# Attention kernel with one in-order DMA queue: three kinds of transfers moved or reordered between SyncE and ScalarE

## The chip, the core and the metric

The kernel runs on one core of one Trainium2 chip. The metric is the device time of one execution in microseconds (us). A measurement of this kernel can tell about 0.5% from no change.

## What is computed

A transformer block on 2 sequences of 1024 rows of width 512, fp32, cut here to its skeleton:

```python
mod = silu(c) @ wmod                      # shift, scale, gate of both halves
h = layernorm(x) * (1 + ca) + sa
q, k, v = h @ Wq, h @ Wk, h @ Wv          # 32 query heads, 8 key/value heads, head size 64
q, k = rope(q), rope(k)
attn = softmax(causal(q @ k.T / 8)) @ v
x = x + ga * (attn @ Wo)
h = layernorm(x) * (1 + cb) + sb
gu = h @ ternary(w_gate_up).T             # ternary weights: per group of 64, sign times scale
x = x + gb * (rms_norm(silu(gate) * up) @ ternary(w_proj).T)
```

## The kernel before

The program has four stages, one after the other, each with its own instruction streams for the five engines: a prologue (layer norm, modulation), `attention`, the output projection and the feed-forward part. The change lies in `attention` (line 343 and following).

`attention` computes one group of 4 query heads and one key/value head at a time, 8 groups (g = 0 to 7). A group has 72 steps (T), and in each step TensorE (PE) does one tile of 128 keys by 4 heads of 128 queries: it turns (transposes) the exponentials (line 698, four of 128 columns), and multiplies, two steps later (`LAG = 2`), the high and low halves with the values (lines 710, 711). In the same steps it projects the next queries, keys and values (lines 656 to 658) and computes scores (lines 688 to 690). The engines are kept in step only by semaphores; each engine's stream is written out by a `step` function, in which every kind of work has a fixed delay in steps behind the event that it belongs to. An engine works strictly through its own stream, so a wait on a semaphore holds back all that stands behind it on that engine.

**Query pieces.** A group needs eight pieces of rotated queries (`X_USES`, kinds `qx` and `qy`). A piece that starts at step s is projected in steps s to s+3; VectorE (DVE) multiplies by cosine and sine at s+4 (lines 835, 836); SyncE (SP) swaps the halves by four transfers at s+5 (`swap`, line 572); GpSimd (POOL) adds at s+6 (line 898); ScalarE (ACT) rounds at s+8 (line 792), POOL takes the rest at s+8 (line 909); SP places the result in `q_hl` by four transfers at s+10 (`place`, line 582). The pieces that the first scores of the next group need start at steps 46 and 51 (here called piece 9 and piece 10, their numbers in `X_USES`), so piece 10 is placed at step 61, and the scores at step 63 wait for it. Piece 11 starts at 56 and is swapped at step 61 too, ahead of the place of piece 10.

**Output blocks.** Each pair of steps' rows gives a large and a small block of outputs, 16 blocks of 4 heads by 128 queries in a group. A block whose last tile is at step e is copied by ACT at e+2 (`copy_out`, line 748), its upper half is shifted to the lower partitions by SP at e+3 (`shift`, line 558), added by POOL at e+5 (line 889), multiplied by the reciprocal denominators by POOL at e+6 (line 894), and stored by SP at e+7 (`store`, line 566). Blocks 10 and 11 end at steps 51 and 53.

**Reciprocals.** For a pair n of blocks, DVE makes the reciprocals at step 9n and turns them at 9n+1; SP saves them to memory at 9n+2 (`save_den`, line 589, four transfers) and loads them spread over 64 partitions into `rd_all` (`spread_den`, line 595) once per block. `rd_all` holds one block. So the load of a block can only start when the block before has been multiplied; the order of SP's stream ensures that, since the load stands right behind the store of the block before, and that store waits for the multiplication.

**Ternary weights.** 6 units in a group: loaded by ACT's queue (line 800), worked on by ACT, DVE and POOL, and stored by SP at 12 steps behind the unit's start (`store_unit`, line 600), after POOL's last operation on it (line 924) at 11.

SP's stream in a step (lines 602 to 622) has the order shift, swap, place, store, save, spread of the large block, spread of the small block behind a store, ternary store, and the weights of the next group once.

Of the kernel before, what the change touches and what calls it, by code (L numbers as in the profile page):

```python
# [20 lines left out]
ALU = mybir.AluOpType  # L21
ACT = mybir.ActivationFunctionType
AX = mybir.AxisListType
F32 = mybir.dt.float32
# [3 lines left out]
P = 128  # L28
B, S, E = 2, 1024, 512
T = B * S  # L30
H, KVH, D = 32, 8, 64
GQ = H // KVH
# [262 lines left out]
LAG = 2  # L295
# [47 lines left out]
def attention(nc, wq, wk, wv, w_gu, w_p, consts_in, w_in, w_raw, cos, sin, mask, ident, hT_hi, hT_lo, ot_dram, rden_dram,  # L343
              tern_gu, tern_p):
    with ExitStack() as ctx:
        sb = lambda n, s, d: ctx.enter_context(nc.sbuf_tensor(n, s, d))
# [15 lines left out]
        p_lo = sb("p_lo", [P, P_RING, 512], F32R)  # L362
        o_sb = sb("o_sb", [P, 2, 512], F32)
        o_low = sb("o_low", [D, 2, 512], F32)
        rd_all = sb("rd_all", [D, 512], F32)
        negm = sb("negm", [P, len(ROWS)], F32)
        den = sb("den", [P, 2, len(ROWS)], F32)
        rd = sb("rd_b", [P, 2, DEN_COLS], F32)
# [163 lines left out]
        def unit_of(g, u, gu, down):  # L532

            if u < 4:
                return gu[bass.ds(g, 1), u].rearrange("g p d -> (g p) d")
            return down[bass.ds(g, 1), u - 4].rearrange("g p r h -> (g p) r h")

        def unit_tile(u, tile):

            return tile[:] if u < 4 else tile[:].rearrange("p (r h) -> p r h", r=2)  # L540
# [9 lines left out]
        @block.sync  # L550
        def _(sp):
            ot_g = ot_dram.rearrange("(g h d) t -> g d h t", g=KVH, h=GQ)
            tern_gu_g = tern_gu.rearrange("(g u p) d -> g u p d", g=KVH, p=P)
            tern_p_g = tern_p.rearrange("(u r p) (g h) -> g u p r h", u=2, p=P, g=KVH)

            def shift(g, n):
                blocks_o.await_(sp, g, n)
                sp.dma_start(o_low[:, n % 2, :], o_sb[D:P, n % 2, :]).then_inc(o_shifted[n % 2], 16)

            def store(g, n):  # L560
                pair, small = divmod(n, 2)
# [29 lines left out]
            def spread_den(g, n):  # L591
                if n % 2 == 0:
                    pairs_out.await_(sp, g, n // 2)
                row = rden_dram[n // 2 % 2, GQ * (n % 2):GQ * (n % 2) + GQ, :].rearrange("(o h) q -> o (h q)", o=1)
                sp.dma_start(rd_all[:], row.broadcast_to([D, GQ * P])).then_inc(rd_in[n % 2], 16)

            def store_unit(g, u):
                to = unit_of(g, u, tern_gu_g, tern_p_g)
                units_tern.await_(sp, g, u)
                sp.dma_start(to, unit_tile(u, w_hat)).then_inc(tern_out, 16)  # L600

            def step(body, T):
                for g, n in body.blocks(T, LAG + 1):
                    shift(g, n)
                for g, n, _ in body.uses(T, 5, kinds=("kv", "qx", "qy")):
                    swap(g, n)
                for g, n, _ in body.uses(T, 10, kinds=("qx", "qy")):
                    place(g, n)
                for g, n in body.blocks(T, LAG + 5):
                    store(g, n)  # L610
                for g, n in body.pairs(T, 2):
                    save_den(g, n)
                for g, n in body.pairs(T, 6):
                    spread_den(g, 2 * n)
                for g, n in body.blocks(T, LAG + 5):
                    if n % 2 == 0:
                        spread_den(g, n + 1)
                for g, u in body.units(T, 12):
                    store_unit(g, u)
                if T == W_LOAD and body.holds(0, 0, KVH - 2):  # L620
                    sp.wait_ge(w_ready, body.g + 1)
                    load_weights(sp, wq, wk, wv, w_raw, w_in, body.g + 1)
# [109 lines left out]
        def _(act):  # L732
# [3 lines left out]
            act.copy(ident_r[:], ident[:]).then_inc(consts_ready, 1)  # L736
            act.copy(mask_r[:], mask[:]).then_inc(consts_ready, 1)

            def high(g, T):
                tiles_t.await_(act, g, T)  # L740
                tiles_pv.await_(act, g, T - P_RING)
                act.copy(p_hi[:, T % P_RING, :], ps[:, T_BANK + T % 2, :]).then_inc(phi_ready, 1)  # L742
# [15 lines left out]
            def step(body, T):  # L758
# [8 lines left out]
                    high(g, t)  # L767
                for g, n in body.blocks(T, LAG):
                    copy_out(g, n)
                for g, r in body.rows(T, 1):  # L770
                    exponentials(g, r)
                for g, n, _ in body.uses(T, 4, kinds=("kv",)):
# [20 lines left out]
                for g, u in body.units(T, 3):  # L793
                    units_in.await_(act, g, u)
                    units_tern.await_(act, g, u - 1)
                    act.activation(w_abs[:], wf[:], ACT.Abs).then_inc(abs_ready, 1)
                    act.activation(w_sign[:], wf[:], ACT.Sign).then_inc(sign_ready, 1)
                for g, u in body.units(T, 0):
                    units_sign.await_(act, g, u - 1)
                    act.dma_start(unit_tile(u, wf), unit_of(g, u, gu_g, wp_g)).then_inc(wf_in, 16)  # L800

            bodies(act, step)

# [76 lines left out]
        def _(pool):  # L881
# [4 lines left out]
            def step(body, T):  # L886
# [4 lines left out]
                for g, n in body.blocks(T, LAG + 4):  # L891
                    blocks_a.await_(pool, g, n)
                    blocks_rd[n % 2].await_(pool, g, n // 2)
                    pool.tensor_tensor(o_sb[0:D, n % 2, :], o_sb[0:D, n % 2, :], rd_all[:], ALU.mult).then_inc(o_scaled, 1)  # L894
                for g, n, _ in body.uses(T, 6, kinds=("kv", "qx", "qy")):
                    rows, buf = D if X_USES[n][0] == "kv" else P, buf_of(n)
                    buf_swap[buf].await_(pool, g, BUF[buf].index(n))
# [662 lines left out]
```

## Time and profile before

| | us |
|---|---|
| median of 3 runs | 2027.5 |
| lowest and highest | 2020.21, 2028.98 |
| the profiled execution | 2022.91 |
| its span, first to last instruction | 2021.1 |
| PE busy | 1783.6 |
| DVE busy | 1277.2 |
| ACT busy | 1148.7 |
| POOL busy | 952.4 |

The mean granted TensorE clock of the profiled execution is 0.961 of full speed (2.4 GHz). The attention stage's matmuls run from about 68 us to 1388 us of the span. "Idle before" in a row is the time in which the engine had nothing to do ahead of the instruction, and the name behind the arrow is what released it. A line's number is that of the kernel before. In rows, SPq and ACTq are the queues of SP and ACT on which transfers are issued; an issue also shows the time its engine's sequencer takes for it.

### The profile page before, as it was taken

The page shows a single profiled execution, that of the slowest core. Times are in us where ns is not written, and L with a number is a line of the kernel's source. Part 1 is how long each engine was busy: PE and PEld are TensorE (multiplying, and loading weights), DVE is VectorE, ACT ScalarE, POOL GpSimd, SP SyncE. Part 2 cuts the span into 40 slices and gives each one's busy share as a digit, 9 for nine tenths or more (in the row PEclk, how much of TensorE's full clock was granted, in tenths as well). Part 3 has the DMA queues.
Part 4 walks back from the last instruction along what each step waited for, and adds up shares of the span by engine and source line. Part 5 has one row for each costly group of instructions (what it writes and reads, how often), then busy time and mean ns, then how long its engine had stood idle before and what let it go on. Part 6 is the DMA issues. An engine that isn't in the chain of part 4 may idle for free. (4 is left out here: it accounts for less than half of the span.)

```text
span 2021.1 us, 28183 instructions
## 1 busy us (share of the span) xinstructions
PE 1783.6 (88%) x9585; PEld 1482.5 (73%) x9585; DVE 1277.2 (63%) x2079; ACT 1148.7 (57%) x2307; POOL 952.4 (47%) x773
## 2 busy tenths in 40 slices
PE   7489989989889989998998998984999789999997
PEld 6267867878778778777877877873788667777776
DVE  6368768768768767776876876884333255454443
ACT  4257767767767767776776776784322244323221
POOL 0235656566556656655665656654000024444443
PEclk9799999999989989999998999997999989999999
DMA  6134344244334434433434334333655300101000
GB/s 247 27 84 111 86 116 105 80 115 112 82 97 111 104 89 105 123 81 103 117 83 118 101 81 117 96 95 118 225 178 190 116 22 1 48 0 48 1 26 22
DMA packets 174921, 190.96 MB, mean 94 GB/s; under 512 B 31408, under 2 KB 117688, under 8 KB 174784
## 3 DMA queue, kind: packets, MB, share of 16 engines
q1 hardware_dynamic: 156992, 164.07, 29.0%
q10 hardware_dynamic: 17792, 25.17, 4.2%
q8 instruction: 73, 1.20, 0.3%
q14 instruction: 64, 0.52, 0.1%
HBM read 86.12 MB, written 31.74 MB: 58 GB/s over the span
## 5 line engine op out<-in xcount | busy, mean ns | idle before, releaser
L812 DVE TENSOR_TENSOR p_lo<-ps_b,p_hi 128x512 fp32r<-128x512 f32 x576 | 395.0, 687 | 181.0 <-ACT p_hi L742 177.0
L742 ACT CAST p_hi<-ps_b 128x512 fp32r<-128x512 f32 x576 | 338.0, 589 | 218.1 <-PE ps_b L698 213.9
L755 ACT ACTIVATE p<-ps_b,negm 128x640 f32<-128x640 f32 (+7 forms) x512 | 382.6, 751 | 127.1 <-DVE negm L820 123.2
L820 DVE TENSOR_REDUCE negm<-ps_b 128x1 f32<-128x640 f32 (+7 forms) x512 | 377.4, 747 | 113.4 <-PE ps_b L690 111.0
L698 PE MATMUL ps_b<-ident,p 128*128 128x128 f32 x2304 | 356.5, 278 | 9.6 <-DVE p_lo L812 3.8
L688 PE MATMUL ps_b<-k_hh,q_hl 128*128 128x512 f32 (+3 forms) x768 | 271.7, 354 | 81.6 <-DMA q_hl<-rot_x 53.0
L710 PE MATMUL ps_b<-p_hi,v_hl 128*128 128x512 f32 x576 | 278.1, 483 | 11.7 <-ACT o_sb L748 11.2
L698 PEld LDWEIGHTS ps_b<-ident,p 128*128 128x128 f32 x2304 | 253.8, 142 | 40.2 <-issue 11.5
L689 PE MATMUL ps_b<-k_l,q_hl 128*128 128x512 f32 (+3 forms) x768 | 260.7, 352 | 0.0
L894 POOL TENSOR_TENSOR o_sb<-o_sb,rd_all 64x512 f32<-64x512 f32 x128 | 163.7, 1279 | 166.9 <-DMA rd_all<-reciprocals 164.9
L688 PEld LDWEIGHTS ps_b<-k_hh,q_hl 128*128 128x128 f32 x768 | 147.9, 193 | 126.5 <-issue 56.2
L711 PE MATMUL ps_b<-p_lo,v_hl 128*128 128x512 f32 x576 | 229.2, 398 | 0.0
L1294 PE MATMUL ps_d<-h_hi,gu 128*128 128x512 f32 x512 | 201.4, 393 | 8.1 <-ACT xn_d L1313 4.6
L1295 PE MATMUL ps_d<-h_lo,gu 128*128 128x512 f32 x512 | 200.0, 391 | 0.0
L656 PE MATMUL ps_b<-hT_hi,w_hi 128*128 128x512 f32 x384 | 159.2, 414 | 45.9 <-DVE v_hl L847 16.3
L898 POOL TENSOR_TENSOR rot_c<-rot_c,rot_x 128x512 f32<-128x512 f32 (+1 forms) x96 | 122.9, 1280 | 151.9 <-DMA rot_x<-rot_s 151.8
L889 POOL TENSOR_TENSOR o_sb<-o_sb,o_low 64x512 f32<-64x512 f32 x128 | 164.2, 1287 | 40.4 <-DMA o_low<-o_sb 40.2
L689 PEld LDWEIGHTS ps_b<-k_l,q_hl 128*128 128x128 f32 x768 | 148.2, 193 | 29.5
L1380 POOL TENSOR_TENSOR sq<-a 128x512 f32<-128x512 f32 x60 | 71.2, 1186 | 179.1 <-DVE a L1462 178.7
L657 PE MATMUL ps_b<-hT_hi,w_lo 128*128 128x512 f32 x384 | 155.5, 405 | 0.0
L658 PE MATMUL ps_b<-hT_lo,w_hi 128*128 128x512 f32 x384 | 153.8, 401 | 0.0
L1462 DVE TENSOR_TENSOR a<-ps_d,sg 128x512 f32<-128x512 f32 x64 | 44.2, 691 | 159.4 <-PE ps_d L1295 140.9
(139 smaller groups left out, 3344.3 us busy)
## 6 DMA issues: line engine op xcount, KB each, us to landing
rot_x<-rot_s SPq DMA_DIRECT2D x320, 64.0 KB, 2.0
q_hl<-rot_s SPq DMA_DIRECT2D x128, 128.0 KB, 2.4
q_hl<-rot_x SPq DMA_DIRECT2D x128, 128.0 KB, 2.4
rd_all<-reciprocals SPq DMA_DIRECT2D x128, 128.0 KB, 3.0
o_low<-o_sb SPq DMA_DIRECT2D x128, 128.0 KB, 2.3
attention_out<-o_sb SPq DMA_DIRECT2D x128, 128.0 KB, 2.4
o_raw<-attention_out SPq DMA_DIRECT2D x32, 512.0 KB, 4.7
wf<-in_L_ffn_w_gate_up ACTq DMA_DIRECT2D x32, 256.0 KB, 3.3
```

The costliest lines, as they stand in the source:

```text
L688: pe.matmul(ps[:, bank, 0:n], q, k_hh[:, unit, k0:k0 + n], start=True, stop=False)
L689: ins = pe.matmul(ps[:, bank, 0:n], q, k_l0[:, unit, k0:k0 + n], start=False, stop=(k0 + n < nk))
L698: ins = pe.transpose(ps[:, T_BANK + T % 2, h * P:(h + 1) * P], p_32[:, parity, h, column * P:(column + 1) * P], ident[:])
L710: pe.matmul(ps[:, O_BANK, :], v_hl[:, unit, j, :], p_hi[:, T % P_RING, :], start=(j == 0), stop=False)
L711: pe.matmul(ps[:, O_BANK, :], v_hl[:, unit, j, :], p_lo[:, T % P_RING, :], start=False, stop=(j == i)).then_inc(pv_done, 1)
L742: act.copy(p_hi[:, T % P_RING, :], ps[:, T_BANK + T % 2, :]).then_inc(phi_ready, 1)
L755: act.activation(p_32[:, parity, h, column * P:column * P + nk], s, ACT.Exp, bias=negm[:, k:k + 1], scale=1.0, accum_out=den[:, parity, k: ...
L812: dve.tensor_tensor(p_lo[:, T % P_RING, :], ps[:, T_BANK + T % 2, :], p_hi[:, T % P_RING, :].bitcast(F32), ALU.subtract).then_inc(plo_read ...
L820: dve.tensor_reduce(negm[:, k:k + 1], s, AX.X, ALU.max, negate=True).then_inc(max_ready, 1)
L889: pool.tensor_tensor(o_sb[0:D, n % 2, :], o_sb[0:D, n % 2, :], o_low[:, n % 2, :], ALU.add).then_inc(o_added, 1)
L1294: pe.matmul(ps[:, bank + half, :], gu[:, m, half, k, :], h_hi[:, parity, k, :], start=(k == 0), stop=False)
L1295: i = pe.matmul(ps[:, bank + half, :], gu[:, m, half, k, :], h_lo[:, parity, k, :], start=False, stop=(k == CT - 1))
```

## The change

`shift` and `store_unit` are moved from SP to ACT: ACT's step issues the shift at the same step (e+3) as before, right behind its `high` and `copy_out`, and the ternary store three steps later (15 instead of 12 behind the unit's start), right behind the two activations that wait for the same unit.
```diff
-        rd_all = sb("rd_all", [D, 512], F32)
+        rd_all = sb("rd_all", [D, 2, 512], F32)
...
         @block.sync
-            def shift(g, n):
-                blocks_o.await_(sp, g, n)
-                sp.dma_start(o_low[:, n % 2, :], o_sb[D:P, n % 2, :]).then_inc(o_shifted[n % 2], 16)
...
                 if n % 2 == 0:
                     pairs_out.await_(sp, g, n // 2)
...
-                sp.dma_start(rd_all[:], row.broadcast_to([D, GQ * P])).then_inc(rd_in[n % 2], 16)
-
-            def store_unit(g, u):
-                to = unit_of(g, u, tern_gu_g, tern_p_g)
-                units_tern.await_(sp, g, u)
-                sp.dma_start(to, unit_tile(u, w_hat)).then_inc(tern_out, 16)
+                blocks_s.await_(sp, g, n - 2)
+                sp.dma_start(rd_all[:, n % 2, :], row.broadcast_to([D, GQ * P])).then_inc(rd_in[n % 2], 16)
 
             def step(body, T):
-                for g, n in body.blocks(T, LAG + 1):
-                    shift(g, n)
                 for g, n, _ in body.uses(T, 5, kinds=("kv", "qx", "qy")):
                     swap(g, n)
                 for g, n, _ in body.uses(T, 10, kinds=("qx", "qy")):
                     place(g, n)
+                for g, n in body.pairs(T, 2):
+                    save_den(g, n)
+                for k in range(2):
+                    for g, n in body.pairs(T, 5 + 2 * k):
+                        spread_den(g, 2 * n + k)
                 for g, n in body.blocks(T, LAG + 5):
                     store(g, n)
-                for g, n in body.pairs(T, 2):
-                    save_den(g, n)
-                for g, n in body.pairs(T, 6):
-                    spread_den(g, 2 * n)
-                for g, n in body.blocks(T, LAG + 5):
-                    if n % 2 == 0:
-                        spread_den(g, n + 1)
-                for g, u in body.units(T, 12):
-                    store_unit(g, u)
...
         @block.scalar
+            def shift(g, n):
+                blocks_o.await_(act, g, n)
+                act.dma_start(o_low[:, n % 2, :], o_sb[D:P, n % 2, :]).then_inc(o_shifted[n % 2], 16)
+
+            def store_unit(g, u):
+                to = unit_of(g, u, tern_gu_g, tern_p_g)
+                units_tern.await_(act, g, u)
+                act.dma_start(to, unit_tile(u, w_hat)).then_inc(tern_out, 16)
...
                 for g, n in body.blocks(T, LAG):
                     copy_out(g, n)
+                for g, n in body.blocks(T, LAG + 1):
+                    shift(g, n)
                 for g, r in body.rows(T, 1):
                     exponentials(g, r)
...
                     act.activation(w_sign[:], wf[:], ACT.Sign).then_inc(sign_ready, 1)
+                for g, u in body.units(T, 15):
+                    store_unit(g, u)
...
         @block.gpsimd
-                    pool.tensor_tensor(o_sb[0:D, n % 2, :], o_sb[0:D, n % 2, :], rd_all[:], ALU.mult).then_inc(o_scaled, 1)
+                    pool.tensor_tensor(o_sb[0:D, n % 2, :], o_sb[0:D, n % 2, :], rd_all[:, n % 2, :], ALU.mult).then_inc(o_scaled, 1)
...
-    nc = bacc.Bacc("TRN2", target_bir_lowering=False, num_devices=1)
+    nc = bacc.Bacc("TRN2", target_bir_lowering=False, num_devices=1, dynamic_dma_scratch_size=4096)
```

The first place is SP's stream from step 58 to step 61 of a group, ahead of the scores at step 63. Before, it reads (L566 block stores, L595 reciprocals, L600 ternary store, L572 swap of piece 11, L582 place of piece 10; in brackets the semaphore that it waits for, `b_o_scaled` being POOL's multiplication):

```order
L566 DMA attention_out<-o_sb 64x4x128 [waits b_o_scaled]
L595 DMA rd_all<-reciprocals 64x512
L566 DMA attention_out<-o_sb 64x4x128 [waits b_o_scaled]
L595 DMA rd_all<-reciprocals 64x512 [waits b_rd_out]
L600 DMA ternary_down<-w_hat 128x2x256 [waits b_t_tern]
L572 DMA rot_x<-rot_s 32x512 [waits b_x_used]
L572 DMA rot_x<-rot_s 32x512 x3
L582 DMA q_hl<-rot_s 64x2x256 [waits b_qlo_ready1]
L582 DMA q_hl<-rot_x 64x2x256
```

Now the same steps read (new line numbers: L560 stores, L590 reciprocals, L566 swap, L576 place):

```order
L560 DMA attention_out<-o_sb 64x4x128 [waits b_o_scaled]
L590 DMA rd_all<-reciprocals 64x512 [waits b_o_scaled,b_rd_out]
L560 DMA attention_out<-o_sb 64x4x128 [waits b_o_scaled]
L566 DMA rot_x<-rot_s 32x512 [waits b_x_used]
L566 DMA rot_x<-rot_s 32x512 x3
L576 DMA q_hl<-rot_s 64x2x256 [waits b_qlo_ready1]
L576 DMA q_hl<-rot_x 64x2x256
```

The load of block 11's reciprocals has gone to step 52, and the ternary store has left the queue; the two block stores still stand ahead of swap and place.

The second place is ACT's stream around a block's copy (here the end of the first pairs of group 0). Before (L742 `high`, L748 `copy_out`, L755 exponentials, L792 rounding):

```order
L792 CAST rot_s<-rot_c 128x512 [waits b_rotated0]
L742 CAST p_hi<-ps_b 128x512 [waits b_pv_done,b_t_ready] x2
L748 COPY o_sb<-ps_b 128x512 [waits b_o_out1,b_pv_done]
L755 ACTIVATE p,den<-ps_b,negm 128x640 [waits b_max_ready]
L742 CAST p_hi<-ps_b 128x512 [waits b_pv_done,b_t_ready]
```

Now (L738, L744, L751, L790 are the same four, L728 is the shift):

```order
L790 CAST rot_s<-rot_c 128x512 [waits b_rotated0]
L738 CAST p_hi<-ps_b 128x512 [waits b_pv_done,b_t_ready]
L728 DMA o_low<-o_sb 64x512 [waits b_o_copied]
L738 CAST p_hi<-ps_b 128x512 [waits b_pv_done,b_t_ready]
L744 COPY o_sb<-ps_b 128x512 [waits b_o_out1,b_pv_done]
L751 ACTIVATE p,den<-ps_b,negm 128x640 [waits b_max_ready]
L738 CAST p_hi<-ps_b 128x512 [waits b_pv_done,b_t_ready]
L728 DMA o_low<-o_sb 64x512 [waits b_o_copied]
```

A shift now stands directly behind a `high` of the step after its block's copy, and waits for ACT's own copy. PE's, DVE's and POOL's streams keep their order.

## Rows read from the trace of the kernel before

**Rows 1.** the page, part 1: busy us, share of the span, instructions

```profile
PE 1783.6 (88%) x9585; PEld 1482.5 (73%) x9585; DVE 1277.2 (63%) x2079; ACT 1148.7 (57%) x2307; POOL 952.4 (47%) x773
```

**Rows 2.** waits of PE: us in total, times, longest us

```profile
PE ps_b L688 <- DMA q_hl<-rot_x: 53.0, 8, 7.9
PE ps_b L688 <- ACT p L755: 28.6, 30, 2.1
```

**Rows 3.** timeline of PE at one stall: start us, us, operation, [idle before]

```profile
256.83 0.40 PE L656 MATMUL ps_b<-hT_hi,w_hi 128*128 128x512 f32 x1
...
264.89 0.77 PE L688 MATMUL ps_b<-k_hh,q_hl 128*128 128x512 f32 x1 [7.21 <-DMA q_hl<-rot_x]
```

**Rows 4.** timeline of PE, the first stall and one behind ACT

```profile
109.65 0.76 PE L688 MATMUL ps_b<-k_hh,q_hl 128*128 128x512 f32 x1 [3.25 <-DMA q_hl<-rot_x]
...
191.94 0.33 PE L688 MATMUL ps_b<-k_hh,q_hl 128*128 128x128 f32 x1 [1.98 <-ACT p L755]
```

**Rows 5.** windows: stretch, us, busy PE, PEld, DVE, ACT, POOL, PEclk, DMA

```profile
265.00:270.00 5.00, 5.00 (x16) 4.16 (x17) 2.62 (x5) 1.80 (x3) 1.26 (x1) 0.54 0.02 3
192.00:196.00 4.00, 3.53 (x23) 3.06 (x24) 2.53 (x5) 3.35 (x9) 0.01 (x1) 1.00 0.28 70
```

**Rows 6.** waits of SP's queue and of POOL

```profile
SPq L566 <- POOL o_sb L894: 214.9, 74, 5.1
...
SPq L600 <- POOL w_hat L924: 61.6, 38, 3.9
...
POOL o_sb L894 <- DMA rd_all<-reciprocals: 164.9, 49, 6.0
```

**Rows 7.** timeline of SP's DMA issues ahead of that stall

```profile
254.90 0.62 SPq L566 DMA_DIRECT2D attention_out<-o_sb  x1
...
257.27 0.41 SPq L600 DMA_DIRECT2D ternary_down<-w_hat  x1
257.73 2.47 SPq L572 DMA_DIRECT2D rot_x<-rot_s  x4
260.24 0.66 SPq L582 DMA_DIRECT2D q_hl<-rot_s  x1
...
262.28 0.61 SPq L582 DMA_DIRECT2D q_hl<-rot_x  x1
```

**Rows 8.** timeline of POOL over the same steps

```profile
253.59 1.28 POOL L894 TENSOR_TENSOR o_sb<-o_sb,rd_all 64x512 f32<-64x512 f32 x1 [2.29 <-DMA rd_all<-reciprocals]
254.84 1.29 POOL L909 TENSOR_TENSOR rot_x<-rot_c,rot_s 128x512 fp32r<-128x512 f32 x1
```

**Rows 9.** timeline of DVE, same steps

```profile
250.56 0.68 DVE L836 TENSOR_TENSOR rot_s<-ps_b,sin 128x512 f32<-128x512 f32 x1
```

**Rows 10.** DMA issues: count, KB each, median us to landing

```profile
rd_all<-reciprocals SPq DMA_DIRECT2D x128, 128.0 KB, 3.0
```

**Rows 11.** lines 558 and 800: count, ns min/median/max

```profile
L558 SPq DMA_DIRECT2D o_low<-o_sb x128: 461/503/1736, 142.6 to 1392.2; - x128
...
L800 ACTq DMA_DIRECT2D wf<-in_L_ffn_w_gate_up x32: 334/347/399, 123.5 to 1331.1; - x32
```

**Rows 12.** timeline of ACT around one issue of its queue

```profile
148.51 0.59 ACT L742 CAST p_hi<-ps_b 128x512 fp32r<-128x512 f32 x1
148.52 0.34 ACTq L800 DMA_DIRECT2D wf<-in_L_ffn_w_gate_up  x1
```

**Rows 13.** timeline of all engines, end of the attention stage

```profile
1385.71 1.28 POOL L894 TENSOR_TENSOR o_sb<-o_sb,rd_all 64x512 f32<-64x512 f32 x1 [3.46 <-DMA rd_all<-reciprocals]
...
1389.53 0.59 ACT L748 COPY o_sb<-ps_b 128x512 f32<-128x512 f32 x1 [2.99 <-DMA attention_out<-o_sb]
...
1397.94 1.25 POOL L894 TENSOR_TENSOR o_sb<-o_sb,rd_all 64x512 f32<-64x512 f32 x1 [2.29 <-DMA rd_all<-reciprocals]
1399.22 0.64 SPq L566 DMA_DIRECT2D attention_out<-o_sb  x1
...
1412.53 0.77 PE L1030 MATMUL ps_c<-wo_hi,o_hi 128*128 128x512 f32 x1 [24.48 <-DVE o_lo L1143]
```

More of the change, by code:

```diff
@@ L552, in _ @@
             ot_g = ot_dram.rearrange("(g h d) t -> g d h t", g=KVH, h=GQ)
-            tern_gu_g = tern_gu.rearrange("(g u p) d -> g u p d", g=KVH, p=P)
-            tern_p_g = tern_p.rearrange("(u r p) (g h) -> g u p r h", u=2, p=P, g=KVH)
-            def shift(g, n):
-                blocks_o.await_(sp, g, n)
-                sp.dma_start(o_low[:, n % 2, :], o_sb[D:P, n % 2, :]).then_inc(o_shifted[n % 2], 16)
             def store(g, n):
@@ L737, in _ @@
             act.copy(mask_r[:], mask[:]).then_inc(consts_ready, 1)
+            tern_gu_g = tern_gu.rearrange("(g u p) d -> g u p d", g=KVH, p=P)
+            tern_p_g = tern_p.rearrange("(u r p) (g h) -> g u p r h", u=2, p=P, g=KVH)
+            def shift(g, n):
[5 more added lines that the diff above has]
+                act.dma_start(to, unit_tile(u, w_hat)).then_inc(tern_out, 16)
             def high(g, T):
```

## The prediction

> **What bounds the kernel now.** I read the page first: PE is busy 1783.6 of 2021.1 us, 88% of the span, and every other engine at most 63% [rows 1]. So only what stops PE counts, or slows it. Next the waits of PE: in the attention stage the largest is the first score matmul of a group waiting for the placed queries, 53.0 us in 8 stalls; behind it comes the wait for exponentials, 28.6 us in 30 stalls of at most 2.1 [rows 2]. Then PE's timeline at one of the eight: PE issues its last three projection matmuls from 256.83 (one every 0.23 us) and then stands 7.21 us until 264.89 [rows 3]. The first of the eight, before any block exists, is 3.25 us [rows 4]; the other seven average (53.0 - 3.25) / 7 = 7.1. The windows show a second price: in the 5 us behind such a stall the granted clock is 0.54 with PE busy all the time, while behind a stall of 1.98 us [rows 4] it is 1.00 [rows 5]. 5 x (1 - 0.54) = 2.3 us of work are lost there.
>
> Why the queries are late is in SP's queue, read backwards from the stall [rows 7]. The last of four place transfers is issued at 262.28 and PE starts 2.61 later. The four are issued from 260.24, behind the four of a swap from 257.73. From the start of the swap to PE's start it is always 2.51 + 2.04 + 2.61 = 7.16 us. The swap's data were there at 250.56 + 0.68 = 251.24 [rows 9], so SP was 6.5 us late. It stood behind a block store until 254.90 and behind a ternary store until 257.27. The block store waited for POOL's multiplication, which began at 253.59 after 2.29 us without work, waiting for the reciprocals [rows 8]; and these could be asked for only once the single buffer was free. Over the span SP waits 214.9 us for that multiplication and 61.6 for the ternary units, and POOL waits 164.9 us for reciprocals [rows 6], whose transfer takes 3.0 [rows 10].
>
> **The change, part by part.**
>
> *Reciprocals early, two buffers.* 128 loads stay 128. Block 11's now starts at step 52 instead of 58, so the multiplication at step 59 finds it. It starts at 253.59 - 2.29 = 251.30 and ends at 252.58 instead of 254.87. Nothing else on POOL changes; the remainder of piece 10 (line 909) ends at about 253.8, before the place needs it. The load's new wait, for the block two before, lies in SP's queue too: the multiplication that it wants is one to five steps older, so I cost it at nothing; what covers it is POOL's slack, and if POOL is late, swap and place are late by the same.
>
> *Ternary store off SP.* It was issued at 257.27, 1.1 us after the store from 254.90 and the load behind it (0.62 us each to issue) were through [rows 7]. On ACT it stands three steps later, right behind an activation that waits for the same unit, so it adds no wait there.
>
> *New start of the swap.* The block store (0.65 us to issue) now follows the multiplication: 252.58 + 0.65 = 253.2. Then PE starts at 253.2 + 7.16 = 260.4. Without the stall PE would start at 264.89 - 7.21 = 257.7. That leaves 2.7 us. Bounded from below by the data alone, 251.24 + 7.16 = 258.4, it leaves 0.7. POOL also waited for reciprocals in the steps before, so the multiplication should come a little sooner than 251.30; I take 2.0. From above, the stall could stay 7.2 if SP still comes late by another wait.
>
> *Sum at the stalls.* 7 x (7.1 - 2.0) = 36 us. A stall of 2.0 is like the one of 1.98 behind which the clock was full [rows 5], so 7 x 2.3 = 16 us of slow clock go too. The first stall of 3.25 has no block or ternary store ahead of it in SP's queue and stays.
>
> *The end of the stage.* The last multiplication but two waited 3.46 us for its reciprocals; the last copy of a block waited 2.99 us for the store behind it; and the last multiplication waited 2.29, before the last store at 1399.22 [rows 13]. The output projection cannot start earlier, its first matmul has 24.48 us of idle ahead. 2.99 + 2.29 = 5 us go; the bounds are 2.3 and 8.
>
> *Shifts and stores on ACT.* 128 shifts at 0.50 us (the median on SP) and 48 ternary stores at 0.41 [rows 7, 11] are 64 + 20 = 84 us of ACT's sequencer, 10 us in a group of some 162. The nearest rows are ACT's own issues of weight loads: 0.35 us [rows 11], issued 0.01 us after a `high` of 0.59 us has started [rows 12], so the issue is over before the engine is. A shift stands in the same place, behind a `high`, and 0.50 is still below 0.59; its semaphore, ACT's own copy of the step before, is long there. I take 3 us for all 176. The bounds are 0 and 84.
>
> *What comes late next.* With the long stall gone, ACT and DVE lose the pause in which they catch up, just where the widest rows (1024 columns) begin. The waits for exponentials are 28.6 / 8 = 3.6 us a group; I let them grow by 1 us a group, 7 us in all. The bounds are 0 and 3.6 x 7 = 25.
>
> The sum is 36 + 16 + 5 - 3 - 7 = 47 us. Against the profiled execution, 2022.9, that is 1976. The median of the three runs, 2027.5, lies 4.6 above that execution, within the spread shown; I put the median after at 1978, a little above the sum.
>
> **A rule that speaks against it.** Of the waits of SP's queue the rows say that 276 us hung on POOL [rows 6] and only parts of a microsecond on each issue. The Trainium skill ("DMA: Bandwidth & Descriptors", section "Issuing engines are not separate DMA queues") says that transfers issued from several engines run on the same 16 DMA engines and that spreading them saves only the sequencer's time to issue. By the rule alone this change would be worth next to nothing; I forecast more because what leaves the queue here is mostly waiting, which the rule does not speak of.
>
> **The rivals.**
>
> A. *Only issue time is saved.* SP stays late by waiting, since the two block stores and a load with a wait still stand ahead of the swap, and only two issues leave steps 58 to 61: at 0.41 and 0.62 us [rows 7] 1.0 us a group, 7 us in all. For it speaks the order of the stream; against it that the multiplication was idle for reciprocals 2.29 us in just this place. It gives 2016, no change that can be told. The rule above would have this outcome. Chance 0.09.
>
> B. *The stall shrinks by half and the clock still falls.* POOL works nearly without a pause in these steps, and a late `save_den` holds the load of step 59 and with it the store. A stall of about 4.5 gives 7 x 2.6 = 18 us, the clock nothing (behind the first stall of 3.25 I cannot exclude it), the end 5 us, ACT -3: 2003. Chance 0.15.
>
> C. *ACT's queue becomes the bound, slower.* If the issue is not hidden, each shift delays the exponentials behind it and the next `high`, and PE waits for both. The price is up to 84 us against the 54 that the rest gives before ACT and the catching up; it decides from 54 / 176 = 0.31 us exposed at each issue. Fully exposed: 2022.9 - 54 + 84 = 2053. For it speaks that PE already waits for exponentials 30 times; against it the hidden issues [rows 12]. Chance 0.08, half exposed (2011) belongs to A or B.
>
> **How the numbers follow.** The forecast has 0.68. About 0.5% (10 us) is what can be told from no change. Forecast and B are faster, 0.83; A and what C leaves in the middle are the same, 0.10; C is slower, 0.07. The range from 1957 (stall 0.7 us, no growth of other waits: 7 x 1.3 + 7 + 3 = 19 us below the sum) to 2008 takes in B and half of the bound on ACT, and leaves out A and C.
>
> **What would show it.** In the profile after: seven waits for the placed queries of 1 to 3 us each, their total with the first 15 to 25 us instead of 53.0; the windows behind them at clock 1.00; POOL's wait for reciprocals near 0; no SP wait for the ternary unit; ACT's waits by PE for exponentials 28 to 45 us; the gap before the output projection 19 instead of 24.5. I am wrong if the waits for queries stay above 35 us, or if PE's waits on ACT grow by more than they fall.

## The result and the profile after

| | before | after |
|---|---|---|
| median, us | 2026.62 | 1993.07 |
| lowest and highest, us | 2020.21, 2028.98 | 1990.73, 1994.04 |
| span of the profiled execution, us | 2021.1 | 1992.2 |

The ratio is 0.9836, 95% interval 0.9824 to 0.9848: 33.6 us faster by the medians, 28.9 by the two spans. The forecast was 1978 with a range of 1957 to 2008. The direction and the place are right, the size was forecast too large.

The page of the kernel after, part 1, against [rows 1]: every engine runs as many instructions as before, and PE's share of the span has risen from 88% to 90%. PE's busy time for the same 9585 matmuls is 4.2 us longer (1783.6 before), which bears on the clock, below.

```profile
PE 1787.8 (90%) x9585; PEld 1487.4 (75%) x9585; DVE 1277.6 (64%) x2079; ACT 1147.7 (58%) x2307; POOL 964.6 (48%) x773
```

The waits of PE over the whole span (us in total, times, longest), against [rows 2]:

```profile
PE ps_b L672 <- ACT p L751: 31.2, 34, 2.2
PE ps_b L672 <- DMA q_hl<-rot_x: 25.5, 8, 4.0
PE ps_c L1030 <- DVE o_lo L1143: 21.7, 2, 19.0
...
PE ps_b L694 <- ACT o_sb L744: 10.1, 20, 1.1
...
PE ps_b L682 <- DVE p_lo L812: 7.5, 12, 1.4
```

The wait for placed queries has halved, 53.0 to 25.5; the wait for exponentials has grown from 28.6 to 31.2, and the gap ahead of the output projection's first matmul is 19.03 instead of 24.48 [rows 13].

The same stall as in [rows 3, 7, 8], one group after the first. First SP's issues (start us, duration, line; new lines: L560 block store, L566 swap, L576 place):

```profile
252.49 0.62 SPq L560 DMA_DIRECT2D attention_out<-o_sb  x1
253.16 2.51 SPq L566 DMA_DIRECT2D rot_x<-rot_s  x4
255.71 0.77 SPq L576 DMA_DIRECT2D q_hl<-rot_s  x1
...
257.86 0.61 SPq L576 DMA_DIRECT2D q_hl<-rot_x  x1
```

POOL in the same steps (L894 multiplication of block 11, L909 remainder of piece 10), which now has no idle ahead of either:

```profile
251.16 1.31 POOL L894 TENSOR_TENSOR o_sb<-o_sb,rd_all 64x512 f32<-64x512 f32 x1
252.42 1.29 POOL L909 TENSOR_TENSOR rot_x<-rot_c,rot_s 128x512 fp32r<-128x512 f32 x1
```

And PE, with the last projection matmul and the first score:

```profile
257.40 0.39 PE L642 MATMUL ps_b<-hT_lo,w_hi 128*128 128x512 f32 x1
261.03 0.77 PE L672 MATMUL ps_b<-k_hh,q_hl 128*128 128x512 f32 x1 [3.23 <-DMA q_hl<-rot_x]
```

The multiplication runs at 251.16 instead of 253.59, the block store goes at 252.49 instead of 254.90, and no ternary store follows. The swap starts at 253.16 instead of 257.73. The stall is 3.23 us instead of 7.21. But the last place is issued at 257.86 and PE starts 3.17 us later, not 2.61 as before.

The windows behind the stalls (stretch, us, busy us of PE, PEld, DVE, ACT, POOL, granted clock, DMA, GB/s), of the kernel after:

```profile
261.00:266.00 5.00, 4.97 (x18) 4.28 (x19) 2.54 (x5) 1.93 (x3) 0.00 (x0) 0.69 0.01 3
...
736.00:741.00 5.00, 4.83 (x14) 4.09 (x15) 2.39 (x4) 1.52 (x3) 0.00 (x0) 0.50 0.00 0
```

The clock is 0.50 to 0.71 in 5 us from the start of the first score in all seven groups; before it was 0.50 to 0.71 too, with 0.50 or 0.51 in five of seven, now in two. So the slow stretch stayed although the stall halved.

The clock also falls at a second place, once in most groups: behind PE's longest wait for exponentials. Here it is in the kernel before and in the kernel after (PE's matmul behind the wait, and the 5 us from its start):

```profile
354.48 0.33 PE L688 MATMUL ps_b<-k_hh,q_hl 128*128 128x128 f32 x1 [1.97 <-ACT p L755]
354.48:359.48 5.00, 5.00 (x24) 4.47 (x25) 3.11 (x6) 3.59 (x9) 2.33 (x2) 0.66 0.20 56
```

```profile
190.97 0.33 PE L672 MATMUL ps_b<-k_hh,q_hl 128*128 128x128 f32 x1 [1.73 <-ACT p L751]
190.97:195.97 5.00, 5.00 (x24) 4.58 (x25) 2.92 (x6) 3.69 (x9) 2.14 (x2) 0.66 0.12 30
```

Before there are seven such waits of 1.96 to 2.10 us, and the clock behind them is 1.00 four times and 0.66 three times. After there are eight of 1.72 to 2.24 us, with 1.00 twice and 0.66 to 0.69 six times.

Over the span, SP's block stores wait 81.8 us for POOL's multiplication instead of 214.9 [rows 6]; the loads' new wait for an older multiplication (recorded at the helper's line, L331) adds 55.7:

```profile
SPq L560 <- POOL o_sb L894: 81.8, 53, 6.7
...
SPq L331 <- POOL o_sb L894: 55.7, 8, 7.5
```

and POOL's group of multiplications has 3.4 us of idle ahead of it, where it waited 164.9 us for reciprocals:

```profile
L894 POOL TENSOR_TENSOR o_sb<-o_sb,rd_all 64x512 f32<-64x512 f32 x128 | 163.9, 1285 | 3.4
```

ScalarE's timeline around two of the issues that it took over (ACTq is the issue, on the same time axis as the operations):

```profile
242.05 0.81 ACT L751 ACTIVATE p<-ps_b,negm 128x640 f32<-128x640 f32 x1
242.19 0.47 ACTq L728 DMA_DIRECT2D o_low<-o_sb  x1
...
256.67 0.59 ACT L738 CAST p_hi<-ps_b 128x512 fp32r<-128x512 f32 x1
256.79 0.44 ACTq L733 DMA_DIRECT2D ternary_down<-w_hat  x1
257.15 0.63 ACT L794 ACTIVATE w_abs<-wf 128x512 bf16<-128x512 f32 x1
```

The shift is issued at 242.19 for 0.47 us, while an exponential of 0.81 runs from 242.05. The ternary store is issued at 256.79 for 0.44 while a copy of 0.59 runs, and the next operation begins 0.48 after that copy began, as it would without. In these rows both are hidden, like the weight loads in [rows 12].

### The profile page after: what moved, and what is told of

Read it like the earlier page. It is cut to its first block and busy times, and to the rows that moved or that the text cites. A ratio compares the mean times of both kernels' runs of the same rounds, so it can differ in the third digit from the quotient of the medians.

```text
span 1992.2 us, 28246 instructions
## 1 busy us (share of the span) xinstructions
PE 1787.8 (90%) x9585; PEld 1487.4 (75%) x9585; DVE 1277.6 (64%) x2079; ACT 1147.7 (58%) x2307; POOL 964.6 (48%) x773
## 5 line engine op out<-in xcount | busy, mean ns | idle before, releaser
L751 ACT ACTIVATE p<-ps_b,negm 128x640 f32<-128x640 f32 (+7 forms) x512 | 381.8, 749 | 135.1 <-DVE negm L820 131.7
L738 ACT CAST p_hi<-ps_b 128x512 fp32r<-128x512 f32 x576 | 337.4, 588 | 190.5 <-PE ps_b L682 186.1
L672 PE MATMUL ps_b<-k_hh,q_hl 128*128 128x512 f32 (+3 forms) x768 | 271.0, 353 | 56.7 <-ACT p L751 31.2
L694 PE MATMUL ps_b<-p_hi,v_hl 128*128 128x512 f32 x576 | 278.5, 484 | 10.4 <-ACT o_sb L744 10.1
L898 POOL TENSOR_TENSOR rot_c<-rot_c,rot_x 128x512 f32<-128x512 f32 (+1 forms) x96 | 124.6, 1298 | 154.5 <-DMA rot_x<-rot_s 148.7
L889 POOL TENSOR_TENSOR o_sb<-o_sb,o_low 64x512 f32<-64x512 f32 x128 | 174.1, 1364 | 25.2 <-DMA o_low<-o_sb 25.0
L894 POOL TENSOR_TENSOR o_sb<-o_sb,rd_all 64x512 f32<-64x512 f32 x128 | 163.9, 1285 | 3.4
L909 POOL TENSOR_TENSOR rot_x<-rot_c,rot_s 128x512 fp32r<-128x512 f32 x64 | 82.2, 1284 | 167.7 <-ACT rot_s L790 167.7
```

The source lines that it names most:

```text
L672: pe.matmul(ps[:, bank, 0:n], q, k_hh[:, unit, k0:k0 + n], start=True, stop=False)
L694: pe.matmul(ps[:, O_BANK, :], v_hl[:, unit, j, :], p_hi[:, T % P_RING, :], start=(j == 0), stop=False)
L751: act.activation(p_32[:, parity, h, column * P:column * P + nk], s, ACT.Exp, bias=negm[:, k:k + 1], scale=1.0, accum_out=den[:, parity, k: ...
```

## The experiments

Twelve kernels were run, each against the kernel before on the same chip. In the table, "queries" is PE's wait for placed queries in the span, "stalls" are the seven behind the first (the first, 2.8 to 4.6 us where there is one, is in "queries" only), "clock" is the granted clock in 5 us from the first score behind them. The chips differ between groups of runs, so kernels are compared by their ratios.

| kernel | median us | ratio, 95% interval | queries us | stalls us | clock |
|---|---|---|---|---|---|
| before | 2026.6 | 1 | 53.0 | 6.7 to 7.9 | 0.50 to 0.71 |
| the change | 1993.1 | 0.9836 (0.9824 to 0.9848) | 25.5 | 2.9 to 4.0 | 0.50 to 0.71 |
| e1 reciprocals only | 2009.2 | 0.9917 (0.9897 to 0.9937) | 38.2 | 4.7 to 5.8 | 0.50 to 0.59 |
| e2 ternary only | 2015.3 | 0.9948 (0.9928 to 0.9969) | 42.8 | 5.2 to 6.4 | 0.54 to 0.69 |
| e3 shift only | 2015.3 | 0.9959 (0.9941 to 0.9977) | 43.8 | 4.6 to 6.7 | 0.50 to 0.67 |
| e12 shift and ternary | 2008.6 | 0.9906 (0.9890 to 0.9922) | 32.7 | 3.6 to 5.6 | 0.50 to 0.68 |
| e4 double issues | 2000.6 | 0.9880 (0.9860 to 0.9900) | 26.9 | 3.2 to 4.2 | 0.50 to 1.00 |
| e5 place first | 2043.4 | 1.0089 (1.0065 to 1.0114) | 40.9 | 3.4 to 4.9, and eight of 1.0 to 1.4 | 0.50 to 0.69, and 1.00 |
| e6 all stores later | 1998.5 | 0.9860 (0.9841 to 0.9879) | 14.5 | 1.4 to 2.4 | 1.00 |
| e7 both | 2056.3 | 1.0149 (1.0129 to 1.0169) | 24.8 | up to 3.2 | 0.66 to 1.00 |
| e8 PE filled | 1984.8 | 0.9799 (0.9779 to 0.9820) | 2.8 | up to 0.9 | 1.00 |
| e9 store 11 later | 1977.5 | 0.9750 (0.9733 to 0.9766) | 13.5 | 1.4 to 1.7 | 1.00 |
| e10 place first at 61 | 1972.0 | 0.9715 (0.9698 to 0.9732) | 10.0 | 1.1 to 2.1 | 1.00, once 0.66 |
| e11 all at 61 | 1975.5 | 0.9736 (0.9721 to 0.9751) | 0.5 | one of 0.5 | 1.00 |

### Which part did it

**e1**, only the reciprocals: in the kernel before, the second buffer, the wait `blocks_s.await_(sp, g, n - 2)`, POOL reading `rd_all[:, n % 2, :]` and

```diff
-                for g, n in body.pairs(T, 6):
-                    spread_den(g, 2 * n)
-                for g, n in body.blocks(T, LAG + 5):
-                    if n % 2 == 0:
-                        spread_den(g, n + 1)
+                for k in range(2):
+                    for g, n in body.pairs(T, 5 + 2 * k):
+                        spread_den(g, 2 * n + k)
```

> Only the two buffers and the early loads; shifts and ternary stores stay on SP. If the multiplication waiting for its reciprocals was half of SP's lateness, the store ahead of the swap goes at about 252.5 instead of 254.9 in the group looked at, the ternary store then follows at about 254.9 (POOL's last operation), and the stall at the scores falls from 7.1 to about 5.5 us; 7 x 1.6 = 11 us, and about 5 us at the end of the stage: 16 us faster. If only the two steps together help: under 5 us faster.

PE's waits:

```profile
PE ps_b L687 <- DMA q_hl<-rot_x: 38.2, 8, 5.8
```

The stalls are 5.0 us on average (5.5 were expected) and the kernel is 0.83% faster (17 us; 16 expected).

**e2**, only the ternary store, and **e3**, only the shifts, on ScalarE: the moves of the change's diff, the rest as before.

```diff
-            def store_unit(g, u):                       # e2, in the sync block
-                for g, u in body.units(T, 12):
-                    store_unit(g, u)
+                for g, u in body.units(T, 15):          # e2, in the scalar block
+                    store_unit(g, u)
-                for g, n in body.blocks(T, LAG + 1):    # e3, in the sync block
-                    shift(g, n)
+                for g, n in body.blocks(T, LAG + 1):    # e3, in the scalar block
+                    shift(g, n)
```

> Only the ternary store moved to ScalarE, three steps later. The swap then starts behind the store of 254.9 and a load, at about 256.2 instead of 257.7: stall 5.6 us, 7 x 1.5 = 10 us faster, nothing at the end. If the ternary store only filled time in which SP had to wait anyway: no change.

> Only the shifts moved to ScalarE. None of them stands between step 58 and the place of step 61, so the stall stays near 7 us and the time within 3 us of before. If ScalarE's issues delay the exponentials (the rival that ends slower), PE's waits for exponentials rise above 28.6 us by 10 us or more and the kernel is slower by as much.

e2 came as expected, 0.52% (10.5 us). e3 did not: 0.41% (8 us, interval 5 to 12) faster where nothing was expected. Its stalls are 4.6 to 6.7 us; in three groups they hardly shrank (6.5 to 6.7). SP's timeline of e3 at the first of the seven stalls, which shrank to 4.65, says how (L591 reciprocals of block 11, L562 store, L596 ternary store, L568 swap), with POOL's multiplication of block 11:

```profile
248.40 0.61 SPq L591 DMA_DIRECT2D rd_all<-reciprocals  x1
253.01 0.62 SPq L562 DMA_DIRECT2D attention_out<-o_sb  x1
...
255.38 0.41 SPq L596 DMA_DIRECT2D ternary_down<-w_hat  x1
255.83 2.48 SPq L568 DMA_DIRECT2D rot_x<-rot_s  x4
```

```profile
251.71 1.28 POOL L894 TENSOR_TENSOR o_sb<-o_sb,rd_all 64x512 f32<-64x512 f32 x1
```

No shift stands between step 58 and the stall. But before, SP spent 3.06 us from 239.47 on two shifts, the second of which waited for ScalarE's copy, ahead of the swap of piece 10, which started at 242.58; in e3 it starts at 240.81. The store and the load of reciprocals behind it are as much earlier (the load at 248.40 instead of 250.06), so the multiplication runs at 251.71 without a wait, where it had stood 2.29 us [rows 8].

e3 also answers what the shifts cost ScalarE: PE's waits for exponentials are 29.5 us (28.6 before), where a rise of 10 or more would have shown the rival.

**e12**, both on ScalarE without the reciprocals, says whether they add.

> The kernel before with shifts and ternary stores on ScalarE, without the second buffer and the early loads. If the three parts add (11 + 9.6 without the 16 of the reciprocals): 2005 to 2008. If shift and ternary store shorten the same wait: 2013 to 2016, like either alone.

```profile
PE ps_b L673 <- DMA q_hl<-rot_x: 32.7, 8, 5.5
```

They add: 0.52 + 0.41 = 0.93%, measured 0.94%. With the 0.83% of e1 the three parts make 1.77%, and the whole change, which also puts the stores last, has 1.64%, the same within the intervals; the stores' new place in the step was not run by itself. So about half of the gain is the reciprocals', and half that of the two kinds of transfers that left the queue.

### Does ScalarE pay for its issues

**e4**: the change, and behind each shift a useless transfer of a constant:

```diff
                 act.dma_start(o_low[:, n % 2, :], o_sb[D:P, n % 2, :]).then_inc(o_shifted[n % 2], 16)
+                blocks_spare[n % 2].await_(act, g, n // 2 - 1)
+                act.dma_start(spare[:, n % 2, :], mask[0:D, :]).then_inc(spare_in[n % 2], 16)
```

> The changed kernel with a second, useless transfer (a copy of a constant) issued by ScalarE behind each shift, 128 more. If an issue is hidden behind the running copy of 0.59 us, a second of 0.4 to 0.5 us is no longer fully hidden: 128 x (2 x 0.47 - 0.59) = 45 us of ScalarE's time, of which PE sees a small part, 0 to 10 us. If issues cost PE their full time, 128 x 0.45 = 58 us slower.

```profile
PE ps_b L676 <- ACT p L757: 33.2, 31, 2.1
PE ps_b L676 <- DMA q_hl<-rot_x: 26.9, 8, 4.2
...
PE ps_b L698 <- ACT o_sb L750: 14.0, 22, 1.4
```

2000.6 against 1993.1 by the medians; by the ratios 0.9880 - 0.9836 = 0.44%, 9 us, 0.07 us for each of 128 issues; and this is a second issue, 128 more on top of those that the change has. PE's waits for exponentials (31.2 to 33.2) and for block copies (10.1 to 14.0) took 6 of it. A price of 0.31 us at each issue, from which ScalarE would have made the change slower, is excluded for the shifts' places; ternary stores were not doubled.

### The clock

**e8**: the change with useless matmuls where PE stands still, ahead of the waits of the first scores of a group:

```diff
+                if k == 0 and first == 0 and unit == 0:
+                    rows_p.await_(pe, g, r - ROW_FREED[k])
+                    for _ in range(12):
+                        pe.matmul(ps[:, S_BANK + ROW_BANK[k], :], w_hi[:, 0, 0:P], hT_hi[:, 0, 0:512], start=True, stop=True)
```

> The changed kernel with 12 useless matmuls of 512 columns (2.8 us) ahead of the first scores of a group, where PE stands for 3.2 us. They cost next to nothing if they only fill the stall. If the granted clock falls because PE stands still there, it stays 1.00 and the 5 us windows behind the stalls lose 0 instead of 1.9 us: 7 x 1.9 = 13 us faster than the changed kernel. If it falls for another reason: the same time or slower by up to 5 us.

```profile
PE ps_b L676 <- ACT p L755: 35.6, 37, 2.2
...
PE ps_b L676 <- DMA q_hl<-rot_x: 2.8, 6, 0.9
```

```profile
260.29:265.29 5.00, 5.00 (x30) 4.33 (x31) 3.73 (x7) 3.18 (x6) 0.53 (x1) 1.00 0.03 8
```

The clock is 1.00 in all seven windows behind the filled stalls, and the kernel is 8 us faster than the change by the medians (0.37% by the ratios) although it does 96 matmuls more. So what makes the clock fall there is PE standing still, and without it about 1 us a group is gained net. The net hides larger parts. Without the filler (2.91 us in seven groups and 3.80 in the first) PE's busy time is 1790.1 - 24.2 = 1765.9 us, 22 less than the change's 1787.8: 13 behind the seven stalls, as expected, 2 behind the first, and about 7 because the clock fell behind only two of the eight long waits for exponentials instead of six. Why it fell less often there was not tested. Against it stand the waits for exponentials, which went from 31.2 to 35.6.

### Making the stall shorter

**e6**, all block stores one step later, and **e5**, place ahead of swap in every step; **e7** has both:

```diff
-                for g, n in body.blocks(T, LAG + 5):    # e6
+                for g, n in body.blocks(T, LAG + 6):
                     store(g, n)
+                for g, n, _ in body.uses(T, 10, kinds=("qx", "qy")):    # e5
+                    place(g, n)
                 for g, n, _ in body.uses(T, 5, kinds=("kv", "qx", "qy")):
                     swap(g, n)
-                for g, n, _ in body.uses(T, 10, kinds=("qx", "qy")):
-                    place(g, n)
```

> The changed kernel with place ahead of swap in SP's step, so the four placing issues of piece 10 no longer stand behind the four swapping issues of piece 11. The place then waits only for POOL's remainder (done at 253.7 in the group looked at, after the block store of 252.5) instead of starting at 255.7: stall 3.2 - 2.0 = 1.2 us, 7 x 2.0 = 14 us. If a stall so short leaves the granted clock at 1.00, up to 13 us more: 1966 to 1980. If the clock falls after it as it does after 3.2 us: 1979.

> The changed kernel with each block store one step later (behind swap and place of step 61 for block 11). The swap then starts when its data are there, at 251.3 instead of 253.2: stall 3.2 - 1.8 = 1.4 us, as in the run before: 1966 to 1980. If POOL's remainder (253.7) is what the place waits for, the same. If the later stores hold back the copies of blocks on ScalarE, PE's waits for o_sb rise above 10 us.

> Both edits. The place waits only for POOL's remainder at 253.7 in either case, so nothing on top of either: stall 1.2 us. If the block store ahead still matters: less than 1.2.

e6 shortened the stalls as expected (most are 1.4 us, the clock is 1.00), but 1966 to 1980 was expected and it was no faster than the change (0.24% slower, at the edge of what the intervals tell):

```profile
PE ps_b L672 <- ACT p L751: 35.1, 36, 2.2
PE ps_b L694 <- ACT o_sb L744: 22.8, 26, 3.0
...
PE ps_b L672 <- DMA q_hl<-rot_x: 14.5, 8, 3.3
```

The waits for block copies went from 10.1 to 22.8. ScalarE's waits name the reason, which is not there in the change:

```profile
ACT o_sb L744 <- DMA attention_out<-o_sb: 19.8, 11, 3.2
```

A block's copy needs the store of the block two before, which now goes up to a step too late.

e5 missed altogether: slower than the kernel before. PE's waits are 44.6 us for block copies and 40.9 for queries:

```profile
PE ps_b L694 <- ACT o_sb L744: 44.6, 35, 4.3
PE ps_b L672 <- DMA q_hl<-rot_x: 40.9, 16, 4.9
```

At the step before the stall place and swap do stand in the other order, but the place starts at 267.44, not sooner, because the piece itself is late (SP's place and swap; POOL's sum, which waited for its swap):

```profile
267.44 0.63 SPq L576 DMA_DIRECT2D q_hl<-rot_s  x1
...
270.09 2.50 SPq L566 DMA_DIRECT2D rot_x<-rot_s  x4
...
260.14 1.30 POOL L898 TENSOR_TENSOR rot_c<-rot_c,rot_x 128x512 f32<-128x512 f32 x1 [2.81 <-DMA rot_x<-rot_s]
```

The swap of piece 10 at step 56 now stands behind the place of piece 9, and behind the swap hang sum, rounding, remainder and place. POOL waits 298.9 us for swapped halves instead of 148.7. The pieces' chain begins at the swap and ends at the place, so the transfer with the longer chain behind it must go first. e7, for which 1.2 us of stall were expected, missed too and adds both harms: 60.8 us of waits for block copies.

**e9** and **e10** keep each edit to the one place where it helps, and **e11** has both and POOL's remainder of piece 10 ahead of the multiplication at step 59:

```diff
                 for g, n in body.blocks(T, LAG + 5):    # e9
-                    store(g, n)
+                    if n != 11:
+                        store(g, n)
+                for g, n in body.blocks(T, LAG + 6):
+                    if n == 11:
+                        store(g, n)
+                if T == 61:                             # e10, ahead of swap
+                    for g, n, _ in body.uses(T, 10, kinds=("qx", "qy")):
+                        place(g, n)
```

> The changed kernel with only block 11's store one step later (step 61, behind swap and place), all others where they are. If the loss of the run with all stores later came from the copies of blocks that wait for their stores (PE's waits for o_sb 22.8 instead of 10.1 us), it goes away here, and the stall of 1.4 us with the clock at 1.00 behind it stays: 7 x (1.8 + 1.9) = 26 us below the changed kernel, 1967. If shortening that stall just moves the loss to the exponentials: 1980 or above.

> The changed kernel with place ahead of swap at step 61 alone. If placing first was harmful because at the other steps it made the swap, with the longer chain behind it (sum, rounding, remainder, place), wait for POOL's remainder, the harm goes and the place starts at 253.7 instead of 255.7: stall 1.2 us, clock 1.00, about 26 us below the changed kernel, 1967. If it is harmful at step 61 too: slower than the changed kernel.

> Both, and POOL's remainder of piece 10 (step 59) ahead of the multiplication of block 11. The remainder can then start when ScalarE's rounding is done, at 251.2 instead of 252.4, the place starts at 252.4: stall below 0.3 us, 7 x 1.1 = 8 us below either alone, 1959.

e10 has the lowest time, 56 us below the kernel before by the medians of the runs made together, 2.85% by the ratio (2.68 to 3.02%); e11's interval overlaps with it. In the seven stalls it is no better than e9 (10.0 against 10.4 us in all). What it has more is the first stall, 3.1 us in e9, which is gone: the first group's pieces are placed at step 61 too, from 101.25 instead of 104.60. SP's issues and PE's waits of e10:

```profile
249.61 0.62 SPq L560 DMA_DIRECT2D attention_out<-o_sb  x1
250.86 0.61 SPq L576 DMA_DIRECT2D q_hl<-rot_s  x1
...
252.81 0.83 SPq L576 DMA_DIRECT2D q_hl<-rot_x  x1
253.69 2.53 SPq L566 DMA_DIRECT2D rot_x<-rot_s  x4
```

```profile
PE ps_b L676 <- ACT p L755: 34.5, 36, 2.2
...
PE ps_b L676 <- DMA q_hl<-rot_x: 10.0, 7, 2.1
...
PE ps_b L698 <- ACT o_sb L748: 9.2, 19, 0.9
```

Each stayed above its forecast (e9 1977 against 1967, e10 1972 against 1967, e11 1975 against 1959). Part of it is the clock's second place: behind the long waits for exponentials it fell in five of eight in e9 and in seven of eight in e10. In e11 the queries come in time (0.5 us of waits), and it is not faster than e10, since

```profile
PE ps_b L680 <- ACT p L759: 42.3, 35, 2.6
...
PE ps_b L702 <- ACT o_sb L752: 15.6, 24, 1.9
```

PE now waits 42.3 us for exponentials and 15.6 for block copies, against 34.5 and 9.2 in e10. Most of the growth lies right behind the first scores: the waits for exponentials in the 20 us that follow them are, over the seven groups, 1.7 us before, 7.1 in the change, 10.7 in e8, 9.5 in e10 and 16.0 in e11. That ScalarE and DVE had used the stall to catch up fits the step from e10 to e11. It does not explain e8, where they had nearly the same pause as in the change; what differed behind it was PE's clock. And e11 brings a wait of its own: ScalarE's copies wait 14.2 us for block stores (0.4 in e9), so e11 does not prove that nothing below can be had.

## Why the prediction was right, and where its sizes were off

*The place.* Seven stalls, one queue, waiting and not issue time: right, by the timelines after and by e1, e2 and e12. Rival A (only issue time, 7 us) is out: the change gave 33.6. The Trainium skill ("DMA: Bandwidth & Descriptors", section "Issuing engines are not separate DMA queues") says that only the sequencer's time to issue is saved. In e2 that would be 7 x 0.41 = 3 us at the stalls, and 10.5 us were gained, since the queue had also stood 1.1 us at the ternary store's semaphore in the group shown [rows 7].

*The start of the swap.* Forecast 253.2, measured 253.16; the multiplication 251.30, measured 251.16. The step holds. The load's new wait, costed at nothing, holds SP for 7.5 us once in each of seven groups and 3.5 once; the swap behind it starts at 233.80 (234.08 before), so there it costs nothing.

*The stall that is left, 2.0 us.* Measured 25.5 - 2.8 (the first) = 22.7, or 3.2 on average. Two things failed. I took 2.0 instead of the 2.7 of the working, in the belief that POOL would be still earlier; it was 0.14. And "from the start of the swap to PE's start it is always 7.16" is not so: it is 7.1 to 7.5 before, and 7.3 to 8.4 after. In four of the seven PE starts 3.1 to 3.2 us behind the last place's issue instead of 2.6. The ternary store's issue stands close ahead of the last place now (256.79 and 257.86), and the distance tells the cases apart. In the change, e4, e8 and e12, where it is 1.06 to 1.09 us (12 groups) PE starts 3.05 to 3.17 behind the last place; where it is 1.16 to 3.90 (15 groups), 2.54 to 2.87. In e9, where the store's issue comes 0.3 to 0.9 us behind the last place's, it is 3.0 to 3.3. In e1 and e3, with the ternary stores on SP, and in e2, with the store's issue 3.4 ahead, it is 2.6. That the two transfers share the DMA engines would explain it, but no run moves the store by that one microsecond alone: the cause stays open. The term was 36 us and is 53.0 - 25.5 = 27.5.

*The clock, 16 us.* This is the step that failed most, and with its sign: it gave nothing back. The step was "a stall of 2.0 is like the one of 1.98, behind which the clock was full", read from one row at 191.94. The same trace has 0.66 behind a wait of 1.97 at 354.48, and so behind three of seven such waits; one row could not carry the term. Two things came of it. Behind the stalls, now 3.2 us, the clock still fell: from the seven windows, the work lost was 5 x (7 - 3.75) = 16 us before and 5 x (7 - 4.44) = 13 after, the sums of the seven clocks being 3.75 and 4.44, so 3 us came. Behind the long waits for exponentials, where the sum had no term, the falls went from three to six, 5 us lost before and 10 after, so 5 us went. PE's busy time for the same matmuls, 4.2 us longer, says the same of the whole span. This is from one profiled execution of each kernel. What was right is that the fall hangs on PE's standing still: e8 shows that filling the stall brings the clock back, and in e6 and e9, with stalls of 1.4 to 2.4 us for queries, it is 1.00 behind all of them.

*The end of the stage, 5 us.* 24.48 to 19.03, 5.4 us.

*ScalarE, 3 us, and what comes next, 7 us.* The waits for exponentials grew by 2.6 and those of PE's turns (transposes) for DVE's low halves (line 812) by 3.7 (3.8 to 7.5), together 6.3. The pause that was lost shows where it was looked for: in the 20 us behind the first scores the waits for exponentials grew by 5.4, and elsewhere they fell. ScalarE's issues are not what costs: with both kinds moved (e12) the waits for exponentials are 28.7, with none moved (e1) 31.9. Rival C, slower by ScalarE's issues, is excluded by e4 and e3. Its threshold was also worked out wrong: the rest gives 36 + 16 + 5 = 57 us and not 54, so it would have been 0.32 us an issue and not 0.31, which decides nothing here.

*The sum.* Over the span PE stands 32.9 us less (all its waits together, 224.4 to 191.5 us) and is busy 4.2 us longer: 28.7, and the spans differ by 28.9. The forecast was 47. Of the 18 missing, 20 are the clock (16 forecast, 4 lost) and 8 the stalls; some 10 came back, 4 from ScalarE and what comes next, the others mostly from small waits that had no term.

*How near it was.* The measured 1993 lies 15 us above the forecast of 1978 and 10 below rival B's 2003, and what happened is rival B's story, the stall halved and the clock still falling, with a stall of 3.2 where B had 4.5. B's reason for it did not come: no late `save_den` held the store. So the place and the mechanism of the stalls were right, and that the total came as near as it did is in part luck, since small waits without a term, some 6 us, made up for a third of what the clock was off.

The sum has no gain for the shifts that leave SP, and e3's expectation says why: none stands in steps 58 to 61. e3 shows 8 us: a queue's lateness is handed on, so the wait of a transfer five steps back counts too.

## What to carry to other kernels

In an in-order queue ask of each wait not what it costs its own transfer but which chain stands behind it; the remedy may be an earlier source (a second buffer), another queue, or another place for the one item that blocks the critical one, and the same swap made everywhere can cost more than it gives at the one place (e5 against e10). A term that can come out at one of two levels, such as a clock that may fall behind a stall, should be forecast at both with a chance, and read from all waits of that length in the trace and not from one: here three of seven spoke against the row that was used. PE's busy time for an unchanged number of matmuls shows at once what the clock did as a whole. Look for what the stall itself hides: the waits for exponentials grew from 28.6 us to 31.2, 34.5 and 42.3 in the change, e10 and e11, most of it right behind the place of the stall.

## What the runs showed of the hardware

- The length of PE's pause alone does not decide whether the clock falls behind it. Behind the change's stalls of 2.9 to 4.0 us the granted clock was 0.50 to 0.71 over 5 us in all seven, and behind stalls for queries of 1.4 to 1.7 us 1.00 (e6, e9). But behind waits for exponentials of 1.72 to 1.74 us it was 0.66 to 0.69 in five of seven (the change) and 1.00 in six of seven (e8); 2.06 us gave 0.66 (e10) and 2.38 us 1.00 (e6); 3.18 and 3.22 us gave 1.00 (e4). What else decides stays open.
- Useless matmuls in a pause keep the clock at 1.00 behind it: all seven filled stalls of e8, against none of seven in the change.
- An issue of a 128 KB transfer on ScalarE takes 0.44 to 0.47 us and, in the rows shown, is hidden behind a running operation; a second one directly behind it cost the kernel 0.07 us on average.
- From the issue of the last place to PE's start it took 2.6 us before. It took 3.05 to 3.17 where ScalarE's queue had issued a store of 128 KB 1.06 to 1.09 us ahead of it, and 2.54 to 2.87 where that distance was 1.16 us or more; the cause is open, see above.
